# Two-layer attention, scan and expert kernel: the scan's weights prepared inside the first chunk's preparation, and a later LayerNorm in the first feed-forward

## The chip, the cores and the metric

The kernel runs on one core of one Trainium2 chip. The metric is device time in microseconds of one launch, the median of several runs. A core has five engines with queues of their own: PE (matmul; PEld is its weight load), DVE (vector), ACT (activations), POOL (GpSimd) and SP, which here only issues DMAs. Each runs its own instruction list in order, and semaphores tie them together.

## The reference, cut to what matters

```python
x = L0_attn_x                                   # (2, 4096, 256)
xn = layernorm(x)
s = attention(xn)                               # one head of 256
g = silu(ffn(xn))                               # 1024 hidden, sign weights times alpha, gelu
x = x + s * g
xn = layernorm(x)
# the scan: h = exp(delta*A)*h + delta*u*B ; y = sum_n h*C, 64 states, 128 channels
y = layernorm(xn) * ln_gamma + ln_beta
left, right = split(y @ W_up + b_up)
left = silu(causal_conv(left))
s = xn + (s6(left) * silu(right)) @ W_down + b_down
# experts: every expert takes its 512 best tokens of 4096, plus a shared expert for all
g = silu(experts(xn) + shared_expert(xn))
x = x + s * g
```

Matrix products run on values split in a high and a low part (three products for one), so each weight is split too.

## The kernel before

The program is a chain of stages, each ended on all five queues by a fence (`Fence`: every queue drains and waits for the others; SP first waits for its DMAs to land): first feed-forward of batch 0 (fence 1), attention of batch 0 (fence 2), the same for batch 1 (fences 3 and 4), the scan's weights (fence 5), the second layer (fence 6), the final combination.

**The first feed-forward** works on groups of 512 tokens. The order of every queue comes from one counter n in `ffn0_order`, one step for each block of 128 hidden units, eight steps for a group; `load(G, s)` is the preparation of group G at its own step s, which runs 22 steps ahead of the group, so s falls on the step (s + 2) mod 8 of the eight. At s = 0 SP loads x. The statistics come at s = 2, 3, 4, 5 (one block of 128 tokens each, line 467), the root on POOL at 6, the normalising (`apply`, line 475) at 9 and 10, POOL's copies (`keep`) at 11, the two rounds of transposes at 13 and 17 with the copies and remainders one and two steps behind (`xt_lo` line 488, `k_lo` line 492). Of a finished group, `after` has DVE's two scalings by alpha (line 513) at steps 3 and 4 of the eight, and POOL's bias (line 548) at step 5. Each hidden block goes PE (line 575), ACT gelu (line 622), ACT upper part (line 615), DVE lower part `h_lo` (line 497), PE output product; three banks hold hidden blocks, so PE's product for block H needs `h_lo` of H - 3. In batch 0 the weights' own preparation is put at steps of the same counter (`LOW_AT`, `M_AT`, `ALPHA1_AT` and so on); ACT's first gelu waits for alpha1, which DVE makes from w1 (lines 322 and 325).

**The scan's weights** (`scan_weights_sync`, `_scalar`, `_gpsimd`, `_tensor`, `_vector`, lines 1070 to 1132) are 16 small loads on SP, one exponential on ACT, a selection matrix on POOL, eight tiny matmuls (beta through W_up) on PE and 18 operations on DVE (taps of the convolution, gamma into W_up, high and low parts).

**The second layer** merges two threads on every queue, the scan and the experts. `layer1_steps` takes one step of the scan and then, on average, `pace.rate` steps of the experts. The scan is `prepare(0)` with 38 steps, and then a loop of 519 turns of two steps each, one turn for one pair of states of one chunk of 512 tokens (an item; 32 items make a chunk, 512 items all). An item is two recurrences (DVE, line 1427), one read-out (DVE, line 1434), two decays (ACT, line 1743), a drive (POOL, line 1514), a broadcast of C (PE, line 1598) and the sum over states (PE, line 1607, two matmuls twice). The preparation of later chunks runs beside the loop. The experts take 3 steps of preparation, 16 shared blocks of 512 tokens started 19 steps apart and 48 steps long, 109 steps of choosing (rate 1.3), then 32 routed blocks of the same shape. A block has transposes at its steps 7 and 8, gate logits at 13 (shared blocks only), gate products at 17 to 20, gelus after them on ACT, up products at 29 to 35 (DVE's `product`, line 2207, four of a block) and down products at 40 to 44. Both threads fill the same two PSUM banks (`layer_bank`) in PE's order.

The rates before are 1.06 for the shared blocks and 1.07 for the routed ones. The experts' preparation on SP loads the three shared weights (six loads of 512 KB), then the gate's weights, then x of block 0; on POOL the split of the gate's weights stands in `prepare` of `moe_gpsimd`, ahead of the scan's LayerNorm root.

## Time and profile before

| | us |
|---|---|
| runs | 5074.54, 5084.83, 5075.91 |
| median | 5075.91 |
| the profiled execution: its time | 5073.2 |
| its span, first to last instruction | 5071.5 |

| engine | busy us | share of the span |
|---|---|---|
| PE | 4421.6 | 87% |
| DVE | 3596.5 | 71% |
| POOL | 2536.6 | 50% |
| ACT | 2522.1 | 50% |

By the timeline the feed-forwards run from 0 to about 180 us and from 1051 to about 1220, the attentions behind them up to 1047 and 2076, the scan's weights from 2078 to 2093, the scan's first preparation from there to 2171, the loop from there to 4968, the combination to 5071. Busy shares are averages over these stages, which have different limits, so each edit has to be read from its own stage. Busy time of PE overlaps the next matmul's start and is not PE at its peak.

### The profile page before, as it was taken

To read this page: it belongs to the slowest core of one execution; us is meant where nothing else is said; L and a number is where in the kernel's file an instruction comes from. 1 tells how busy PE (TensorE), PEld (TensorE's weight loads), DVE (VectorE), ACT (ScalarE), POOL (GpSimd) and SP (SyncE) were. 2 spreads that over 40 slices of the span, in tenths; PEclk is the share of its full clock that TensorE was granted. 3 is DMA by queue.
4 is the path that set the end of the run, shared out by engine and by line. 5 is a ranking of instruction groups with operands and counts; after the bars stand their busy time and mean duration, and the time that the engine had idled before them with its cause. 6 is when DMAs were issued, how large, how long until landed. Compare 5 with 4: busy or idle time off the path is not lost. (4 is left out here: it accounts for less than half of the span.)

```text
span 5071.5 us, 63742 instructions
## 1 busy us (share of the span) xinstructions
PE 4421.6 (87%) x22534; PEld 3243.6 (64%) x22534; DVE 3596.5 (71%) x5059; ACT 2522.1 (50%) x4773; POOL 2536.6 (50%) x1838
## 2 busy tenths in 40 slices
PE   7899999968999999599999747789998899998972
PEld 6788888857888888466666424556665566665530
DVE  6466666654666666378777899888878778877795
ACT  5544444445444444366666422256665566566542
POOL 3122222232222200166655616788888889888870
PEclk9999999988999999799999968899999999999996
DMA  2022222220122200144333311265555555655546
GB/s 77 33 83 84 84 84 83 78 75 32 67 84 84 79 22 22 55 141 139 126 125 128 126 37 64 77 191 159 173 172 175 148 165 173 186 158 159 141 155 277
DMA packets 270465, 573.15 MB, mean 113 GB/s; under 512 B 37185, under 2 KB 156226, under 8 KB 270146
## 3 DMA queue, kind: packets, MB, share of 16 engines
q1 hardware_dynamic: 245570, 535.51, 31.5%
q0 software_dynamic: 24576, 33.57, 3.8%
q8 instruction: 178, 2.92, 0.2%
q14 instruction: 141, 1.16, 0.1%
HBM read 446.16 MB, written 122.81 MB: 112 GB/s over the span
## 5 line engine op out<-in xcount | busy, mean ns | idle before, releaser
L1514 POOL TENSOR_TENSOR scan_drive_sb<-scan_b_wide_sb,scan_du_sb 128x1024 f32<-128x1024 f32 x512 | 1289.8, 2547 | 450.8 <-DVE scan_h_sb L1427 438.0
L1427 DVE TENSOR_TENSOR_SCAN scan_h_sb<-decay_bank,scan_state_sb,scan_drive_sb 128x512 f32<-128x512 f32 x896 | 1116.6, 1268 | 105.2 <-ACT decay_bank L1743 104.8
L1607 PE MATMUL y_bank<-scan_ch_sb,identity_sb 128*128 128x512 f32 x2048 | 1082.3, 623 | 0.4 <-DVE scan_temp_sb L1440 0.4
L1743 ACT ACTIVATE decay_bank<-scan_delta_sb,a_neg_sb 128x512 f32<-128x512 f32 x1024 | 701.2, 687 | 496.8 <-DVE scan_h_sb L1427 494.3
L1434 DVE TENSOR_TENSOR scan_ch_sb<-c_pair,scan_h_sb 128x1024 f32<-128x1024 f32 x512 | 615.4, 1202 | 136.2 <-PE c_pair L1598 135.4
L957 PE MATMUL ybank<-v_low_hi_lo_sb,pt_hi_b_sb 128*128 128x384 f32 x2048 | 663.3, 358 | 21.9 <-DVE pt_lo_b_sb L837 16.0
L837 DVE TENSOR_TENSOR pt_lo_b_sb<-pt,pt_hi_b_sb 128x512 fp32r<-128x512 f32 x512 | 352.9, 690 | 413.8 <-ACT pt_hi_b_sb L1000 413.8
L958 PE MATMUL ybank<-v_low_hi_lo_sb,pt_lo_b_sb 128*128 128x256 f32 x2048 | 572.3, 279 | 0.0
L991 ACT ACTIVATE p_b_sb<-scores,softmax_cols_b_sb 128x1024 f32<-128x1024 f32 x256 | 286.0, 1117 | 550.2 <-DVE softmax_cols_b_sb L831 410.8
L1598 PE MATMUL c_pair<-scan_cc_sb,select_state_sb 128*128 128x512 f32 x1024 | 386.9, 460 | 147.0 <-DVE scan_ch_sb L1434 145.5
L1000 ACT ACTIVATE pt_hi_b_sb<-pt 128x512 fp32r<-128x512 f32 x512 | 306.1, 598 | 413.6 <-PE pt L945 413.6
L1607 PEld LDWEIGHTS y_bank<-scan_ch_sb,identity_sb 128*128 128x128 f32 x2048 | 391.3, 198 | 142.6 <-issue 72.9
L957 PEld LDWEIGHTS ybank<-v_low_hi_lo_sb,pt_hi_b_sb 128*128 128x128 f32 x2048 | 383.7, 187 | 92.2 <-DVE pt_lo_b_sb L837 80.9
L958 PEld LDWEIGHTS ybank<-v_low_hi_lo_sb,pt_lo_b_sb 128*128 128x128 f32 x2048 | 385.3, 188 | 0.0
L1598 PEld LDWEIGHTS c_pair<-scan_cc_sb,select_state_sb 128*128 128x128 f32 x1024 | 178.5, 199 | 290.0 <-DVE scan_ch_sb L1434 249.7
L900 POOL TENSOR_TENSOR acc_b_sb<-acc_b_sb,g_in_b_sb 128x256 f32<-128x256 f32 x64 | 47.4, 741 | 631.4 <-DVE acc_b_sb L873 631.4
L945 PE MATMUL pt<-identity_sb,p_b_sb 128*128 128x128 f32 x2048 | 316.4, 277 | 14.5 <-ACT p_b_sb L991 13.7
L945 PEld LDWEIGHTS pt<-identity_sb,p_b_sb 128*128 128x128 f32 x2048 | 240.9, 140 | 135.0 <-ACT p_b_sb L991 89.4
L825 DVE TENSOR_REDUCE softmax_cols_b_sb<-scores 128x1 f32<-128x1024 f32 x256 | 310.7, 1214 | 8.9 <-PE scores L924 8.9
L2371 PE MATMUL layer_bank<-moe_xt_hi_sb,expert_hi_sb 128*128 128x512 f32 x512 | 294.3, 575 | 16.4 <-DVE scan_yt_lo_sb L1382 8.4
L2118 POOL TENSOR_TENSOR moe_h_lo_sb<-moe_g_sb,moe_h_hi_sb 128x512 fp32r<-128x512 f32 x192 | 266.3, 1389 | 64.5 <-ACT moe_h_hi_sb L2049 64.5
L2166 POOL DMA_INDIRECT moe_scratch<-moe_out_sb,moe_rows_sb x128 | 204.9, 1601 | 110.5 <-ACT moe_out_sb L2073 81.5
(313 smaller groups left out, 9762.1 us busy)
## 6 DMA issues: line engine op xcount, KB each, us to landing
scan_b_wide_sb<-b_scratch SPq DMA_DIRECT2D x512, 512.0 KB
w_hi_scratch<-split_hi_sb SPq DMA_DIRECT2D x51, 512.0 KB, 2.8
w_lo_scratch<-split_lo_sb SPq DMA_DIRECT2D x51, 512.0 KB, 4.1
expert_hi_sb<-w_hi_scratch SPq DMA_DIRECT2D x48, 512.0 KB
expert_lo_sb<-w_lo_scratch SPq DMA_DIRECT2D x48, 512.0 KB
x_b_sb<-x SPq DMA_DIRECT2D x16, 512.0 KB, 3.9
g_scratch<-g_out_b_sb SPq DMA_DIRECT2D x16, 512.0 KB, 3.0
split_raw_sb<-WgT SPq DMA_DIRECT2D x16, 512.0 KB, 5.2
```

The source lines that it names most:

```text
L825: e.tensor_reduce(v[:, 0, c:c + 1], k.scores[i % 2][:, :], AX_X, ALU.max, negate=True).then_inc(k.s_chunk_max, 1)
L837: e.tensor_tensor(k.pt_lo[n % 2][:, :], k.pt[n % 2][:, :], f32(k.pt_hi[n % 2][:, :]), ALU.subtract).then_inc(k.s_pt_lo, 1)
L945: turned = e.transpose(k.pt[n % 2][:, j * P:(j + 1) * P], k.p[i % 2][:, kb * P:(kb + 1) * P], consts.identity[:, :])
L957: e.matmul(k.y_bank[:, 0:D + P], k.pt_hi[n % 2][:, cols], kv.v[:, block, :], start=(kb == 0), stop=False, skip_group_check=True)
L958: last = e.matmul(k.y_bank[:, 0:D], k.pt_lo[n % 2][:, cols], kv.v[:, block, 0:D], start=False, stop=(kb == KEY_BLOCKS - 1), skip_group_che ...
L1000: e.activation(k.pt_hi[n % 2][:, :], k.pt[n % 2][:, :], ACT.Copy).then_inc(k.s_pt_hi, 1)
L1427: e.tensor_tensor_scan(k.h[i % H_BUFFERS][:, j, :], k.decay_banks[S % DECAY_BANKS][:, :], k.drive[i % DRIVE_BUFFERS][:, j, :], start, ALU. ...
L1434: e.tensor_tensor(k.ch[i % CH_BUFFERS][:, :, :], k.c_bank[:, :, :], k.h[i % H_BUFFERS][:, :, :], ALU.mult).then_inc(k.s_ch, 1)
L1514: e.tensor_tensor(k.drive[i % DRIVE_BUFFERS][:, :, :], k.b_wide[i % B_BUFFERS][:, :, :], k.du[c % 2][:, :].unsqueeze(1).broadcast_to([P, P ...
L1598: last = e.matmul(k.c_bank[:, j, :], wt.select[:, n:n + 1].broadcast_to([P, P]), k.cc[c % 2][:, :], start=True, stop=True)
L1607: e.matmul(k.y_bank[:, :], consts.identity[:, :], k.ch[i % CH_BUFFERS][:, j, :], start=(n == 0), stop=(n == STATES - 1)).then_inc(k.s_y, 1)
L1743: e.activation(k.decay_banks[S % DECAY_BANKS][:, :], k.delta[c % 2][:, :], ACT.Exp, scale=wt.a[:, n:n + 1]).then_inc(k.s_decay, 1)
```

## The change

In the first feed-forward the LayerNorm of a group is done later and in two pieces instead of four; of batch 0, three steps of the weights' preparation move, alpha1 among them, seven steps ahead. The fence behind the scan's weights goes; their loads are issued at the scan's step 1, behind x of chunk 0, the gate's weights, x of block 0 and the first shared weight; POOL's part stands at step 0, PE's and ACT's at step 9, DVE's at step 10, with a new semaphore `s_made` on which PE's first W_up product and ACT's first use of b_up wait. While chunk 0 is prepared, each step of the scan is followed by two steps of the experts, not 1.06: 76 in all instead of 40. The rates behind it become 1.0. The raw weights get room of their own. POOL splits the gate's weights at step 11 of block 0.

```diff
-LN_STATS_AT = (2, 3, 4, 5)
-LN_RSTD_AT = 6
-LN_APPLY_AT = (9, 10)
-KEEP_AT = 11
-TURN0_AT = 13
+LN_STATS_AT = (8, 9)
+LN_RSTD_AT = 10
+LN_APPLY_AT = (12, 13)
+KEEP_AT = 13
+TURN0_AT = 14
-LOW_AT = -15
-M_AT = -14
+LOW_AT = -13
+M_AT = -12
-ALPHA1_AT = -2
+ALPHA1_AT = -9
...
+WEIGHTS_AT = 9
+def after_part(c, s, leads=False):
+    if c > 0:
+        return 1
+    if leads:
+        return 2
+    return 1 if s == 0 else 3 if s == PREPARE_STEPS - 1 else 2
...
     def prepare(c):
         for s in range(PREPARE_STEPS):
+            if c == 0 and s == WEIGHTS_AT + 1:
+                scan_weights_vector(e, w, wt, k.y_bank, consts)
...
-            yield
+            yield from no_steps(after_part(c, s))
...
-SHARED_RATE = 1.06
-MOE_RATE = 1.07
+SHARED_RATE = 1.0
+MOE_RATE = 1.0
...
     def prepare():
+        e.dma_start(k.gate_raw[:, :, :], a["gateT"].rearrange("(c p) n -> p c n", p=P)).then_inc(k.s_gate_raw, 16)
+        load(0)
         for kind in range(3):
             for half, slot in enumerate((k.ws_hi[kind], k.ws_lo[kind])):
                 e.dma_start(f32(slot[:, :]), w_dram[half][3 * EXPERTS + kind]).then_inc(k.s_ws[kind], 16)
             yield
-        e.dma_start(k.gate_raw[:, :, :], a["gateT"].rearrange("(c p) n -> p c n", p=P)).then_inc(k.s_gate_raw, 16)
...
     def shared(q, s):
+        if q == 0 and s == LOGITS_AT - 2:
+            gate_weights()
...
-            scan_weights_vector(e, w, w1, y_bank, consts)
+            layer1_steps(scan_vector(e, w, scan, fills, w1, consts), moe_vector(e, w, moe, fills, pace), pace)
             fence.compute(e, w, 5)
-            layer1_steps(scan_vector(e, w, scan, fills, w1), moe_vector(e, w, moe, fills, pace), pace)
-            fence.compute(e, w, 6)
```

## Rows read from the trace of the kernel before

**Rows 1.** Timeline, batch 1 of the feed-forward: start us, length us, instruction, [idle before].

```profile
1112.96 0.40 PE L575 MATMUL ffn_bank<-xt_hi_b_sb,sign_sb 128*128 128x512 f32 x1
...
1114.72 2.80 DVE L475 TENSOR_SCALAR x_b_sb<-x_b_sb,ln_moments_sb,ln_rstd_sb 128x256 f32<-128x256 f32 x2
...
1114.84 0.40 PE L575 MATMUL ffn_bank<-xt_hi_b_sb,sign_sb 128*128 128x512 f32 x1
...
1114.89 2.48 POOL L548 TENSOR_TENSOR g_out_b_sb<-g_out_b_sb,b_sb 128x1024 f32<-128x1024 f32 x1 [8.04 <-DVE g_out_b_sb L513]
...
1118.91 0.51 PE L575 MATMUL ffn_bank<-xt_hi_b_sb,sign_sb 128*128 128x512 f32 x1 [2.03 <-DVE h_lo_b_sb L497]
```

**Rows 2.** One line's instructions, line 475: duration ns min/median/max, first and last start.

```profile
L475 DVE TENSOR_SCALAR x_b_sb<-x_b_sb,ln_moments_sb,ln_rstd_sb x64: 394/405/2478, 9.2 to 1179.1; 128x256 f32<-128x256 f32 x64
```

**Rows 3.** Waits by total, whole span: total us, times, longest.

```profile
PE ffn_bank L575 <- DVE h_lo_b_sb L497: 37.4, 18, 3.3
```

**Rows 4.** Timeline, the first 30 us, batch 0: PE, ACT, DVE and SP.

```profile
22.95 0.78 PE L575 MATMUL ffn_bank<-xt_hi_b_sb,sign_sb 128*128 128x512 f32 x1
...
25.68 1.28 ACT L622 ACT_TABLE_LOAD   x1 [6.20 <-DVE alpha_sb L325]
...
17.00 0.67 DVE L488 TENSOR_TENSOR xt_lo_b_sb<-ffn_bank,xt_hi_b_sb 128x512 fp32r<-128x512 f32 x1
...
23.06 2.31 DVE L322 TENSOR_REDUCE alpha_sb<-g_out_b_sb 128x4 f32<-128x1024 f32 x2
...
29.92 0.69 DVE L497 TENSOR_TENSOR h_lo_b_sb<-ffn_bank,h_hi_b_sb 128x512 fp32r<-128x512 f32 x1 [3.80 <-ACT h_hi_b_sb L615]
...
3.75 2.06 SPq L297 DMA_DIRECT2D b_sb<-b  x1
```

**Rows 5.** DMA issues, 0 to 20 us: count, KB each, median us from issue to landing.

```profile
b_sb<-b SPq DMA_DIRECT2D x1, 4.0 KB, 9.6
```

**Rows 6.** Timeline around the fences: SP, POOL and PE.

```profile
2078.01 0.38 SPq L1074 DMA_DIRECT2D gamma_sb<-ln_gamma  x1
...
2093.03 0.38 SPq L1332 DMA_DIRECT2D scan_xn_sb<-xn_scratch  x1
...
2105.02 0.22 POOL L2110 TENSOR_SCALAR gate_hi_sb<-gate_raw_sb 128x32 fp32r<-128x32 f32 x1 [26.11 <-DMA gate_raw_sb<-gateT]
...
2109.94 1.09 PE L1542 MATMUL layer_bank<-identity_sb,scan_xn_sb 128*128 128x128 f32 x4 [20.77 <-ACT scan_xn_sb L1639]
```

**Rows 7.** Busy us of each engine by stretch (count), then PE's granted clock, DMA share, GB/s.

```profile
2078.00:2093.00 15.00, 1.84 (x8) 1.78 (x8) 4.46 (x16) 0.26 (x1) 0.62 (x3) 0.50 0.20 42
2093.00:2171.00 78.00, 45.93 (x213) 35.26 (x214) 11.01 (x25) 38.27 (x76) 22.02 (x20) 0.72 0.29 100
2200.00:2800.00 600.00, 569.05 (x2459) 390.80 (x2458) 466.21 (x478) 386.93 (x820) 363.92 (x205) 0.96 0.40 129
...
3400.00:4800.00 1400.00, 1289.26 (x5199) 852.73 (x5198) 1114.53 (x1116) 874.06 (x1610) 1195.20 (x736) 0.97 0.56 166
4860.00:4968.00 108.00, 78.35 (x203) 34.75 (x204) 106.41 (x93) 43.91 (x89) 67.59 (x30) 1.00 0.40 134
```

**Rows 8.** Groups by line, 2200 to 2800 us: count, busy us, mean ns, idle before.

```profile
L1607 PE MATMUL y_bank<-scan_ch_sb,identity_sb 128*128 128x512 f32 x446 | 236.5, 616 | 0.0
L1434 DVE TENSOR_TENSOR scan_ch_sb<-c_pair,scan_h_sb 128x1024 f32<-128x1024 f32 x112 | 134.9, 1204 | 33.6 <-PE c_pair L1598 33.5
...
L1598 PE MATMUL c_pair<-scan_cc_sb,select_state_sb 128*128 128x512 f32 x222 | 86.3, 472 | 5.5 <-DVE scan_ch_sb L1434 5.2
...
L2207 DVE TENSOR_TENSOR moe_g_sb<-layer_bank,moe_g_sb 128x512 f32<-128x512 f32 x48 | 32.8, 684 | 26.1 <-PE layer_bank L2373 25.7
```

**Rows 9.** Groups by line, 3400 to 4800 us, DVE.

```profile
L1434 DVE TENSOR_TENSOR scan_ch_sb<-c_pair,scan_h_sb 128x1024 f32<-128x1024 f32 x268 | 322.5, 1203 | 98.1 <-PE c_pair L1598 97.3 <-DVE scan_h_sb L1427 0.4
```

**Rows 10.** Groups by line, 4860 to 4968 us, the end of the loop.

```profile
L1434 DVE TENSOR_TENSOR scan_ch_sb<-c_pair,scan_h_sb 128x1024 f32<-128x1024 f32 x30 | 35.8, 1194 | 0.0
```

**Rows 11.** Timeline, DVE, 2150 to 2172 us: the first recurrence.

```profile
2171.18 3.45 DVE L1427 TENSOR_TENSOR_SCAN scan_h_sb<-decay_bank,scan_drive_sb 128x512 f32<-128x512 f32 x3 [11.62 <-ACT decay_bank L1743]
```

More of the change, by code:

```diff
@@ L462, in ffn0_vector, with statistics @@
 def ffn0_vector(e, w, k, wt, kv, b):
-    def statistics(G, j):
+    def statistics(G, half):
         x = k.x[G % X_BUFFERS]
@@ L478, in load @@
     def load(G, s):
-        j, half = part(LN_STATS_AT, s), part(LN_APPLY_AT, s)
-        if j is not None:
-            statistics(G, j)
+        first, half = part(LN_STATS_AT, s), part(LN_APPLY_AT, s)
+        if first is not None:
+            statistics(G, first)
         if half is not None:
@@ L1059, in __init__ @@
         self.s_scaled = self.sem("gamma_in_up")
[L1060 to L1066 removed]
+        self.s_made = self.sem("made")
+        self.raw_up = self.sb("up_raw", [P, DC, D])
+        self.raw_delta = self.sb("wdelta_raw", [P, INNER])
+        self.raw_bc = self.sb("bc_raw", [P, 2, 2, STATES])
+        self.raw_down = self.sb("down_raw", [P, D])
+        self.raw_select = self.sb("select_raw", [P, STATES])
 def scan_weights_sync(e, w, k, a):
@@ L1131, in scan_weights_vector @@
     w.wait_ge(k.s_select, 3)
-    e.tensor_copy(k.select[:, :], k.raw_select[:, :])
+    e.tensor_copy(k.select[:, :], k.raw_select[:, :]).then_inc(k.s_made, 1)
 class Fills(Stage):
@@ L1416, in prepare @@
                 c_lower(c)
-            yield
+            yield from no_steps(after_part(c, s))
     def recur(S):
@@ L1493, in prepare @@
         for s in range(PREPARE_STEPS):
+            if c == 0 and s == 0:
+                scan_weights_gpsimd(e, w, wt)
             if s == STATISTICS_AT[1] + 1:
@@ L1506, in prepare @@
                 delta_u(c)
-            yield
+            yield from no_steps(after_part(c, s))
     def drive(i):
@@ L1547, in up @@
             fills.wait_emptied(w, "turned", c, ci)
+        w.wait_ge(wt.s_made, 1)
         bank = fills.take(w, what, c)
@@ L1574, in prepare @@
         for s in range(PREPARE_STEPS):
+            if c == 0 and s == WEIGHTS_AT:
+                scan_weights_tensor(e, w, wt, k.y_bank)
             ci = part(TURNED_AT, s)
@@ L1589, in prepare @@
                 b_and_c(c, 1)
-            yield
+            yield from no_steps(after_part(c, s, True))
     def broadcast_c(i):
@@ L1656, in left @@
         fills.wait_filled(w, "left", c)
+        w.wait_ge(wt.s_made, 1)
         w.wait_ge(k.s_head, c - c // CHUNKS)
@@ L1713, in prepare @@
         for s in range(PREPARE_STEPS):
+            if c == 0 and s == WEIGHTS_AT:
+                scan_weights_scalar(e, w, wt)
             half, ci = part(APPLY_AT, s), part(TURNED_AT, s - 1)
@@ L1736, in prepare @@
                 c_upper(c)
-            yield
+            yield from no_steps(after_part(c, s))
     def decay(S):
@@ L1926, in shared @@
     def shared(q, s):
-        if s == 0:
+        if s == 0 and q > 0:
             load(q)
@@ L2181, in routed @@
             scatter(q, j)
-    yield from moe_order(pace, prepare(), shared, choose(), routed)
+    yield from moe_order(pace, prepare_steps(), shared, choose(), routed)
 def moe_vector(e, w, k, fills, pace):
@@ L2589, in scalar @@
                 fence.compute(e, w, 2 + 2 * b)
-            scan_weights_scalar(e, w, w1)
+            layer1_steps(scan_scalar(e, w, scan, fills, w1), moe_scalar(e, w, moe, fills, pace), pace)
             fence.compute(e, w, 5)
-            layer1_steps(scan_scalar(e, w, scan, fills, w1), moe_scalar(e, w, moe, fills, pace), pace)
-            fence.compute(e, w, 6)
             combine_scalar(e, w, combine)
@@ L2616, in gpsimd @@
                 fence.compute(e, w, 2 + 2 * b)
-            scan_weights_gpsimd(e, w, w1)
+            layer1_steps(scan_gpsimd(e, w, scan, fills, w1, consts), moe_gpsimd(e, w, moe, fills, consts, pace, xn_dram, acc_dram), pace)
             fence.compute(e, w, 5)
-            layer1_steps(scan_gpsimd(e, w, scan, fills, w1, consts), moe_gpsimd(e, w, moe, fills, consts, pace, xn_dram, acc_dram), pace)
-            fence.compute(e, w, 6)
         def sync(e):
```

48 lines of the change are left out of this document (20 added, 28 removed).

## The prediction, made before the changed kernel ran

> **What bounds the kernel now.** I read three views in this order. The timeline around each edited place shows what waits for what. The busy time by stretch [rows 7] shows what each stage is bound by. The groups by line in the same stretches [rows 8 to 10] give how many items and blocks go through.
>
> In the first feed-forward PE should run without a pause and waits 18 times for `h_lo`, 37.4 us in all [rows 3]. One such wait is in rows 1: DVE's second pair of normalisings, two instructions, takes 2.80 us from 1114.72, while POOL's bias runs from 1114.89 to 1117.37. The pair ends 0.15 us behind POOL's instruction, `h_lo` stands behind it on DVE, and PE idles 2.03 us. The usual time of one normalising is 0.405 us, the longest 2.478 [rows 2].
>
> Between 2078.0, when the fence behind the attention opens, and 2109.9, PE does eight tiny matmuls [rows 6, 7]. The scan's weights take 15.0 us of it. Then POOL's split of the gate's weights waits until 2105.02 for a load that SP issued behind six loads of 512 KB, and the LayerNorm of chunk 0 is queued behind that split. From 2093 to 2171 PE is busy 45.9 us of 78. The first recurrence starts at 2171.18, behind a wait of 11.62 us for ACT's decay [rows 11].
>
> In the loop beside shared experts (2200 to 2800) PE is busy 95% and DVE 78%; beside routed ones (3400 to 4800) PE 92%, POOL 85%, DVE 80%; in the tail, where the experts are done, DVE 99% [rows 7]. One item takes 600/112 = 5.36 us, 1400/268 = 5.22 us and 108/30 = 3.6 us there [rows 7 to 10].
>
> **Part 1: LayerNorm order.** Nothing is added or removed; operations move on DVE, POOL, ACT and PE. Normalising was on steps 3 and 4 of the eight, right behind the alpha scaling whose end releases POOL's bias. It goes to steps 6 and 7. A step is 1.88 us where PE is full: its hidden products start at 1112.96 and 1114.84 [rows 1]. The bias starts about 1.3 us into step 4 (behind `h_lo` and the scaling, 0.6 us each) and lasts 2.48, so it ends near 3.8 us; the first normalising comes behind `h_lo` of step 6, at 3.76 + 0.6 = 4.4 us. It clears by half a microsecond. The long form occurs ten times, five in each batch, as in rows 1, and the PE waits behind them are four of 2.0 to 2.1 and one of 1.3 in either batch: 19.1 us in all, of the 37.4 in rows 3.
>
> What is late next: statistics now stand in pairs (1.06 us) on steps 2 and 3, beside `xt_lo` (0.6) and a scaling (0.6). With `h_lo` (0.6) DVE has 2.26 us for a step of 1.88 twice in a row, so `h_lo` is 0.4 and then 0.8 us late. The path from PE through both ACT operations and `h_lo` back to PE has about 0.5 us to spare (one and a half steps, 2.8 us, against 2.3). I put 0.35 us on each of some 14 groups: 5 us back. Net -14; bounds 0 back (-19) and 0.8 us for each group (-8). The silu pairs, other causes of waits in rows 3, stay.
>
> The lock on SBUF ports weighs here. The Trainium skill ("SBUF — State Buffer", section "SBUF: two separate sides") says that DVE's two-port modes and GpSimd share one port pair as an exclusive lock, and that whichever starts first holds it for its whole instruction. The rows above agree with that; by this rule the half microsecond of clearance decides, and if the bias still starts first the gain of part 1 is zero instead of 14 (a rival below).
>
> **Start of batch 0.** PE's first hidden product starts at 22.95 and ACT's first gelu only at 25.68, when alpha1 is made; the first `h_lo` is at 29.92 [rows 4]. DVE made alpha1 from 23.06 because that is its place in the order; its last input landed at 3.75 + 9.6 = 13.3 us [rows 4, 5]. Moved, it runs from 13.4 to 15.9. It holds back `xt_lo` of group 0, which could start at 14.3 but in the old order ran at 17.0 behind statistics of group 1 that waited for x; now it ends at 16.6 instead of 17.7. Then two statistics, `k_lo` at 19.3, and PE's first product near 19.4. Behind it stand the transposes of group 1, now one step later, waiting for its normalising at 21.7. The third gelu comes 3 us earlier. I take -3, bounds 0 and -4.5. In batch 1, where alpha1 exists and x is the only wait, the product starts some 2 us earlier but the transposes behind it take that back: 0, within 1. Part 1 in all: -17, from -8 to -22.
>
> **Part 2: fence, weights and double pace.** Removed: a fence, and 15 us in which nothing but the weights ran [rows 7]. Added to the preparation: the same 16 loads on SP (issues of 0.45 us each, 7.5 us), ahead of only two of the three shared weights, which block 0 needs at its steps 29 and 40, far later; and the weights' 18 DVE operations, 4.5 us busy, on an engine that is busy 11 of 78 us there. New waits: PE stands at its step 9 until the last load lands, about 2090, with the logits of block 0 already done; `s_made` is set near 2096 and PE needs it at step 15, after 2100. Both are short. SP's xn load moves from 2093.0 to 2078.0, and gate weights no longer wait for 3 MB, so PE's first work, transposes of block 0, can start near 2083 instead of 2109.9.
>
> The experts' steps done by the first recurrence go from 48 to 84: 36 steps, 36/19 = 1.9 blocks. PE's price of a block: of 569 us busy in the shared stretch, items take 236.5 + 86.3; the rest is 246 us for 48/4 = 12 blocks, 20.5 us each [rows 7, 8]. So PE's work in the preparation is 45.9 + 1.9 x 20.5 = 85 us. Before, PE started at 2110 and idled 15 us up to 2171. With the same 15 us of idle time the first recurrence comes at 2083 + 85 + 15 = 2183. No idle time gives 2168, idle time that grows with the work (28 us) 2196. I take 2182, +11 on 2171, bounds -3 and +25. The scan is late and the experts are ahead.
>
> **Part 3: what that is worth in the loop.** Let a be what one more item costs while experts run beside it. A shared block with its 19/1.06/2 = 8.96 items costs 8.96 x 5.36 = 48.0 us, so a block alone 48.0 - 8.96a. Taking 1.9 blocks out saves 91.0 - 17.0a. The loop steps beside experts are counted from the schedule. Shared: before 336/1.06 - 38 = 279 steps (139.5 items), after 336 - 76 = 260 (130). Choosing: 109/1.3 = 84 (42 items) in both. Routed: before 637/1.07 = 595 (297.7 items), after 637 (318.5). Together 479 items before, 490.5 after: 11.4 items move from the tail, at 3.6 us, to a. The sum is 11.4(a - 3.6) - (91.0 - 17.0a) = 28.4a - 132.
>
> For a there are two near rows. If PE sets the pace, a is an item's PE time, (236.5 + 86.3)/112 = 2.88 us [rows 8]: -50. If DVE does, it is the tail's 3.6 [rows 7, 10]: -30. PE is fuller in both stretches, but the 20% idle time of DVE is partly a wait for the broadcast (97 us in 1400, rows 9), and POOL at 85% is near. I take 3.3: -38. The Trainium skill ("Perfetto Trace Analysis", section "Identifying the Most-Contended Engine") calls matmul busy time a poor measure of PE's load and takes weight-load time instead. That is 65% and 61% in these stretches, so PE would not be the limit and DVE's 3.6 would stand. The time by that is 5040; I give it a quarter of the forecast's chance, since PE's waits in rows 8 are short.
>
> **Sum.** -17 + 11 - 38 = -44 on the profiled execution's 5073.2 (span 5071.5): 5029. The median of the runs lies 2.7 us above it, so I forecast 5032.
>
> **Rivals.**
>
> A. Slower: the loop's order, not an engine's load, sets the time of a step, so that an item beside experts costs the same 5.36 us whatever fewer expert steps it carries. With a = 5.36 part 3 is +20 and the time 5076 + 20 + 11 - 17 = 5090. The place is the routed stretch, with 20.8 items more at 5.22 against the tail's 3.6. It decides from a = 4.86 on (28.4a - 132 + 11 - 17 = 0), where the sum is zero. Against it: no row shows an idle PE there (92 to 95%), which a fixed step time needs. For it: ACT and DVE waits for each other on every second item. Chance 0.09.
>
> B. The collision of normalising and bias only moves: `h_lo` late on steps 2 and 3 pushes the bias into step 6. Part 1 gives -3 instead of -17: 5046. For it: clearance of 0.5 us. Against: PE's pace sets both steps. Chance 0.14.
>
> C. The preparation is bound by ACT, not PE: 38 us busy of 78 before, and 1.9 blocks more bring up to 1.9 x 387/12 = 61 us [rows 7], with a table load of 1.28 us at each change of function [rows 4] beside the softplus. PE would idle 23 us more than I allow: first recurrence at 2205, +34 instead of +11, 5055. Chance 0.15.
>
> D. The rates of 1.0 spread the experts' work evenly and PE's stalls fall: 1% of 2100 us, 5011. It is in the forecast's own range. The forecast with it holds 0.62.
>
> **How the numbers follow.** Best ends: -22 - 3 - 50 = -75, 5000. Worst ends: -8 + 25 - 30 = -13, 5063. From 4998 to 5063 the range leaves out A and a part of C. The measurement tells a difference from 0.2%, 10 us, so faster means below 5066: the forecast, B and most of C, 0.87. Same: 0.05. Slower: 0.08, nearly all of A.
>
> **What the profile would show.** Line 475 has no duration over 1 us between 60 and 180 us and between 1090 and 1200, and PE's wait for `h_lo` falls from 37 to about 20 us; if the maximum stays near 2.5, B holds. The first `h_lo` is near 27. SP's xn load comes right behind the fence at about 2060 (part 1 earlier), PE's first expert transposes 5 us behind it, and the first recurrence 104 us behind the fence instead of 93. Over 120 it is C. In the loop an item takes about 5.2 us in the shared stretch and 5.1 in the routed one (fewer expert steps each); if both stay at 5.36 and 5.22, it is A. The last expert product is followed by about 30 items instead of 42. The prediction is wrong if a is outside 2.9 to 3.6, or if the even rate meets the scan's order badly, which no row can show.

## The result, and the profile after

The changed kernel takes 5009.39 us (median, 5004.19 to 5017.5), the kernel before 5080.37 beside it (5074.54 to 5090.1): a ratio of 0.986, 95% interval 0.9836 to 0.9884, or 71 us. I had forecast 5032, in a range from 4998 to 5063. The profiled execution took 5004.19 (span 5002.3) against 5073.2 (span 5071.5): 69 us for the two profiles, with which I compare below.

The first feed-forward. One line's instructions (duration ns min/median/max) and, from the waits of the whole span (total us, times, longest), PE's wait for `h_lo`:

```profile
L476 DVE TENSOR_SCALAR x_b_sb<-x_b_sb,ln_moments_sb,ln_rstd_sb x64: 402/407/414, 9.3 to 1162.3; 128x256 f32<-128x256 f32 x64
...
PE ffn_bank L576 <- DVE h_lo_b_sb L498: 19.6, 9, 3.3
```

Line 476 is the normalising, line 475 before. Its longest was 2478 ns [rows 2] and is now 414; PE's wait for `h_lo` fell from 37.4 us in 18 pauses [rows 3] to 19.6 in 9. The timeline shows the new order of a group, with the place of the bias in it:

```profile
1101.05 0.68 DVE L514 TENSOR_TENSOR g_out_b_sb<-ffn_bank,alpha_sb 128x512 f32<-128x512 f32 x1
...
1101.96 2.42 POOL L549 TENSOR_TENSOR g_out_b_sb<-g_out_b_sb,b_sb 128x1024 f32<-128x1024 f32 x1
...
1104.52 0.73 DVE L476 TENSOR_SCALAR x_b_sb<-x_b_sb,ln_moments_sb,ln_rstd_sb 128x256 f32<-128x256 f32 x2
```

The bias ends at 1104.38, 0.14 us ahead of the normalising; over the ten groups in which the two are neighbours the distance is 0.10 to 0.52 us. In rows 1 the two began 0.17 us apart. PE's busy time between the first and the last `h_lo` of batch 1, before and after (columns as in rows 7: start and end, length, busy us of PE, PEld, DVE, ACT, POOL, then the granted clock):

```profile
1074.30:1221.10 146.80, 128.64 (x792) 115.10 (x792) 87.59 (x155) 101.00 (x157) 45.63 (x47) 0.95 0.12 37
```

```profile
1061.10:1196.80 135.70, 124.67 (x792) 111.06 (x792) 79.04 (x164) 101.99 (x159) 47.03 (x50) 0.99 0.13 40
```

The same 792 matmuls take 4 us less of busy time, at a granted clock of 0.99 and not 0.95. At the start of batch 0 (the views of rows 4, here of the changed kernel) alpha1 is made from 13.43 and the first `h_lo` comes at 25.79 instead of 29.92:

```profile
13.43 2.34 DVE L322 TENSOR_REDUCE alpha_sb<-g_out_b_sb 128x4 f32<-128x1024 f32 x2 [2.72 <-DMA b_sb<-b]
...
19.35 0.80 PE L576 MATMUL ffn_bank<-xt_hi_b_sb,sign_sb 128*128 128x512 f32 x1 [1.59 <-DVE k_lo_sb L493]
...
25.79 0.69 DVE L498 TENSOR_TENSOR h_lo_b_sb<-ffn_bank,h_hi_b_sb 128x512 fp32r<-128x512 f32 x1 [4.21 <-ACT h_hi_b_sb L616]
```

The preparation, timeline of SP, POOL, PE and DVE (the views of rows 6 and 11):

```profile
2054.35 0.37 SPq L1345 DMA_DIRECT2D scan_xn_sb<-xn_scratch  x1
...
2056.85 0.45 SPq L1074 DMA_DIRECT2D gamma_sb<-ln_gamma  x1
...
2062.52 0.22 POOL L2135 TENSOR_SCALAR gate_hi_sb<-gate_raw_sb 128x32 fp32r<-128x32 f32 x1
...
2059.82 1.94 PE L2360 MATMUL layer_bank<-identity_sb,moe_x_sb 128*128 128x128 f32 x8 [11.69 <-DMA moe_x_sb<-xn_scratch]
...
2175.81 2.34 DVE L1444 TENSOR_TENSOR_SCAN scan_h_sb<-decay_bank,scan_drive_sb 128x512 f32<-128x512 f32 x2 [10.94 <-ACT decay_bank L1768]
```

SP's first issue behind the attention comes at 2054.35 instead of 2078.01, POOL's split of the gate's weights no longer waits 26 us for its load, and PE's first transposes come 5.5 us behind SP's first issue, not 32. But the first recurrence comes 121.5 us behind that issue, where it had been 93.2. By stretch (columns as in rows 7: length, busy us of PE, PEld, DVE, ACT, POOL, then the granted clock): the preparation, the shared stretch, the routed one and the tail:

```profile
2054.00:2176.00 122.00, 94.23 (x459) 77.05 (x459) 25.68 (x58) 66.12 (x141) 32.69 (x31) 0.84 0.27 89
2200.00:2800.00 600.00, 562.48 (x2395) 383.21 (x2394) 477.20 (x491) 385.40 (x812) 376.62 (x213) 0.97 0.40 130
3400.00:4780.00 1380.00, 1282.46 (x5161) 839.51 (x5160) 1145.31 (x1135) 883.66 (x1629) 1210.77 (x741) 0.98 0.57 170
4803.00:4898.00 95.00, 67.89 (x173) 29.59 (x172) 92.41 (x80) 38.99 (x80) 59.87 (x26) 1.00 0.41 134
```

Groups by line for the read-out of an item, in 2200 to 2800, 3400 to 4800 and 4803 to 4898 us (the views of rows 8 to 10): 115 items instead of 112, 283 instead of 268, and DVE's idle time in front of them 71.2 us in the routed stretch instead of 98.1.

```profile
L1451 DVE TENSOR_TENSOR scan_ch_sb<-c_pair,scan_h_sb 128x1024 f32<-128x1024 f32 x115 | 138.5, 1204 | 36.2 <-PE c_pair L1620 36.1
...
L1451 DVE TENSOR_TENSOR scan_ch_sb<-c_pair,scan_h_sb 128x1024 f32<-128x1024 f32 x283 | 340.3, 1202 | 71.2 <-PE c_pair L1620 70.7
...
L1451 DVE TENSOR_TENSOR scan_ch_sb<-c_pair,scan_h_sb 128x1024 f32<-128x1024 f32 x27 | 32.1, 1190 | 1.1 <-PE c_pair L1620 1.1
```

**Every stage of every run.** The table is read from the timelines. "FFN" is from the first to the last `h_lo`, both batches added. "Fence" is SP's first issue behind the last attention, "prep" from there to the first recurrence. The loop is cut where ACT empties the last bank of the shared experts, and the first and the last of the routed ones; behind the stroke stand the items read out in that stretch. "Tail" is the rest of the 512 items. All in us, one profiled execution each.

| kernel | first h_lo | FFN | fence | prep | shared | choosing | routed | tail | span |
|---|---|---|---|---|---|---|---|---|---|
| before | 29.9 | 298.2 | 2078.0 | 93.2 | 712 / 134 | 506 / 63 | 1444 / 276 | 135 / 39 | 5071.5 |
| after | 25.8 | 278.9 | 2054.4 | 121.5 | 644 / 124 | 519 / 64 | 1464 / 296 | 96 / 28 | 5002.3 |
| e1_ln_only | 25.0 | 281.7 | 2056.7 | 93.0 | 714 / 134 | 507 / 63 | 1444 / 276 | 135 / 39 | 5053.2 |
| e2_rates_only | 29.8 | 299.2 | 2083.2 | 98.6 | 738 / 143 | 510 / 64 | 1457 / 296 | 27 / 9 | 5018.2 |
| e3_old_rates | 25.9 | 280.4 | 2057.5 | 127.6 | 602 / 115 | 506 / 63 | 1445 / 276 | 210 / 58 | 5052.2 |
| e4_moe_092 | 24.9 | 285.1 | 2061.9 | 121.9 | 643 / 124 | 524 / 66 | 1538 / 322 | none | 4992.6 |
| e5_uneven | 25.8 | 280.4 | 2057.2 | 122.8 | 646 / 124 | 517 / 64 | 1493 / 296 | 96 / 28 | 5035.7 |
| e6_moe_103 | 25.6 | 282.8 | 2059.4 | 125.9 | 646 / 124 | 517 / 64 | 1450 / 287 | 127 / 37 | 5030.9 |
| e7_moe_096 | 25.8 | 284.9 | 2062.0 | 123.9 | 646 / 124 | 524 / 65 | 1508 / 309 | 45 / 14 | 5013.1 |
| e8_collide | 25.7 | 286.4 | 2066.1 | 124.2 | 643 / 124 | 519 / 64 | 1467 / 296 | 96 / 28 | 5020.1 |
| e9_collide_bias | 25.8 | 334.4 | 2110.1 | 124.5 | 643 / 124 | 516 / 64 | 1470 / 296 | 96 / 28 | 5064.0 |
| e10_single_pace | 25.4 | 282.7 | 2057.2 | 82.0 | 741 / 143 | 510 / 64 | 1456 / 296 | 27 / 9 | 4978.4 |
| e11_alpha_late | 26.7 | 286.2 | 2062.4 | 124.3 | 646 / 124 | 517 / 64 | 1470 / 296 | 96 / 28 | 5018.9 |
| e12_warm | 25.8 | 282.7 | 2058.9 | 119.6 | 645 / 124 | 516 / 64 | 1467 / 296 | 96 / 28 | 5006.1 |

How far one profile can be trusted is in the table too: the feed-forward of the changed order, identical in eight of the kernels (after, e3 to e7, e10, e12), lasts 278.9 to 285.1 us, the fence of the old order comes at 2078.0 in before and at 2083.2 in e2, and the preparation at double pace 119.6 to 127.6 (the longest at the rate of 1.06, with 4 expert steps more in it). A difference under 5 us in one stage means nothing.

Against before, the loop gained 68 in the shared stretch and 39 in the tail, and lost 13 in the choosing and 20 in the routed stretch: 74 us. The feed-forwards and the start gave 24, and the preparation took 28.

### The profile page after: what moved, and what is told of

Read it like the earlier page. It is cut to its first block and busy times, and to the rows that moved or that the text cites. A ratio compares the mean times of both kernels' runs of the same rounds, so it can differ in the third digit from the quotient of the medians.

```text
span 5002.3 us, 63736 instructions
## 1 busy us (share of the span) xinstructions
PE 4413.1 (88%) x22534; PEld 3233.9 (65%) x22534; DVE 3570.6 (71%) x5059; ACT 2524.3 (50%) x4773; POOL 2539.3 (51%) x1838
## 5 line engine op out<-in xcount | busy, mean ns | idle before, releaser
L889 POOL TENSOR_SCALAR split_hi_sb<-split_raw_sb 128x512 fp32r<-128x512 f32 x102 | 63.5, 622 | 388.8 <-DMA split_raw_sb<-WgT 123.6
```

## The experiments

Each was timed against the kernel before on the same chip. Medians in us; the intervals of the ratio are 95%.

| kernel | median | ratio to before | interval |
|---|---|---|---|
| e1_ln_only | 5060.13 | 0.9956 | 0.9939 to 0.9973 |
| e2_rates_only | 5028.47 | 0.9903 | 0.9886 to 0.9919 |
| e3_old_rates | 5053.08 | 0.9946 | 0.993 to 0.9963 |
| e4_moe_092 | 4998.23 | 0.9843 | 0.9826 to 0.9859 |
| e5_uneven | 5038.28 | 0.9913 | 0.9896 to 0.9929 |
| e6_moe_103 | 5030.35 | 0.9897 | 0.9881 to 0.9914 |
| e7_moe_096 | 5010.5 | 0.9855 | 0.9838 to 0.9871 |
| e8_collide | 5021.52 | 0.9877 | 0.986 to 0.9893 |
| e9_collide_bias | 5059.81 | 0.9945 | 0.9929 to 0.9962 |
| e10_single_pace | 4980.64 | 0.9793 | 0.9777 to 0.9809 |
| e11_alpha_late | 5015.65 | 0.9858 | 0.9841 to 0.9875 |
| e12_warm | 5008.44 | 0.9852 | 0.9835 to 0.9868 |

The profile of after left two theories to tell apart. The feed-forward had gained 24 us and not 17: was the collision of the normalising with POOL's bias its cause at all? And the routed stretch had taken 20 items more for 20 us, where I had put 3.3 us on each: was that the rate, or something that came with the preparation?

### Part by part

**e1_ln_only**: the first three blocks of the diff and the pair statistics, on the kernel before.

```diff
-LN_STATS_AT = (2, 3, 4, 5)
+LN_STATS_AT = (8, 9)
...
-LN_APPLY_AT = (9, 10)
+LN_APPLY_AT = (12, 13)
...
-ALPHA1_AT = -2
+ALPHA1_AT = -9
```

> The kernel before with the LayerNorm order alone (statistics in pairs, normalising on steps 6 and 7, transposes a step later, the start of the alphas). If part 1 is independent of the rest, the whole of the 24 us by which the attention of batch 1 ended earlier in the changed kernel comes back here: attention ends at 2038 to 2039, the total is 24 us below the kernel before, 5049 on a profiled 5073. If the gain of the later parts leans on it, or if the 24 us hold something of the other parts, it is the predicted 17 or less.

The fence comes 21 us earlier and nothing behind it changes (preparation 93.0, the loop's stretches within 2 us). The time falls by 0.44%, 22 us (18 between the profiles). Part 1 is independent of the rest, and 24 us is the upper end of what one profile shows: over the profiles with this order the fence lies 16 to 24 us ahead of before's 2078.0.

**e2_rates_only**: on the kernel before.

```diff
-SHARED_RATE = 1.06
-MOE_RATE = 1.07
+SHARED_RATE = 1.0
+MOE_RATE = 1.0
```

> The kernel before with both rates at 1.0, everything else as it was. Shared: 298 steps instead of 279, 9.5 items more; routed 637 instead of 595, 20.8 more; the tail 30.3 fewer at 3.5 us. As predicted (one more item beside experts costs 3.3 us whatever the stretch): -6 to -9 us in all. By what the changed kernel's milestones show (20 routed items more at 1.0 us each): shared -3, routed and tail 20.8 x (1.0 - 3.5) = -52, together -55. If the low price needs the preparation or the weights of the changed kernel, it is near the first number.

It gives 0.97%, 49 us (53 between the profiles), near the second of the two forecasts. So two constants bring over two thirds of the change's gain, without the preparation or the weights. The shared stretch takes 9 items more for 26 us, 2.8 each; the routed one 20 more for 13, 0.65 each; the tail, 30 fewer, is 108 us shorter, 3.6 for each. By this the shared rate is worth some 7 us and the routed one some 59; `SHARED_RATE` alone was not run.

**e3_old_rates**: the reverse edit on the changed kernel.

> The changed kernel with the rates of before, 1.06 and 1.07. The reverse of the run with the rates alone: +6 to +9 us on the changed kernel if an item beside experts costs 3.3 us (5015), +55 if a routed one costs 1.0 us (5062). The preparation stays as it is in the changed kernel, first recurrence at 2176, since its steps do not hang on the rate of the stretch that follows, apart from one block's steps.

5053, with the routed stretch back at 1445 us for 276 items. The profile also isolates part 2: this kernel is e1 with the weights and the double pace inside, and the two spans are 5053.2 and 5052.2. The preparation is 34.6 us longer, the shared stretch 112 shorter with 19 items fewer, the tail 76 longer with the same 19 items. All of part 2 together is worth nothing that can be measured at these rates (ratios 0.9956 and 0.9946). The reverse edit costs 0.86%, 44 us, between its two forecasts of 6 to 9 and 55.

### What a routed item costs

**e4_moe_092, e6_moe_103, e7_moe_096**: `MOE_RATE` alone, on the changed kernel.

```diff
-MOE_RATE = 1.0
+MOE_RATE = 0.92
```

> The changed kernel with the routed rate at 0.92 instead of 1.0: 637/0.92/2 = 346 items beside routed experts instead of 318, 28 more, and none left in the tail. Smooth price of 1.0 us for an item more (the time is in the experts' steps, items are nearly free): 28 x (1.0 - 3.4) = -67 us on the changed kernel, 4940. Price of 3.3 us as predicted: -3, 5004. Even rate theory (only a whole number of expert steps for each item avoids stalls, at 1.0 exactly, worth the 48 us by which the routed stretch beat the forecast): the stalls come back, +48 - 3 = +45, 5052.

> The changed kernel with the routed rate 1.03: 637/1.03/2 = 309 items instead of 318.5, 9.3 fewer beside routed experts and as many more in the tail. Linear between 1.07 and 1.0 (either a fixed loss for each step with two expert steps, or a bound by the experts' own chain): routed stretch 1464 - 9.3 x 0.9 = 1456, tail +32, kernel about +24 on the changed one, 5033. If only exactly 1.0 is good (the order of items and expert steps in a fixed phase): 1464 - 28 + 48 = 1484, kernel about +52, 5061. At one price of 3.3 us: +1.

> The changed kernel with the routed rate 0.96: 637/0.96/2 = 332 items, 13.3 more beside routed experts, 13.3 fewer in the tail of 28. Between 1.0 and 0.92 the stretch grew by 74 us for 26 items, 2.85 each. On that line: 1464 + 38 = 1502, tail -45, kernel -7, 5002. If leaving exactly 1.0 costs a fixed amount and the line from there is flatter, the stretch is above 1510 and the kernel above the changed one, over 5010.

The routed stretch by rate: 1.07, 1444 us with 276 items; 1.03, 1450 with 287; 1.0, 1464 with 296; 0.96, 1508 with 309; 0.92, 1538 with 322. Below 1.0 an item more costs (1538 - 1464)/26 = 2.85 us. That is PE's work for an item, 2.88 by rows 8, the lower of my two ends. (If the steps without an expert step, which come with a rate below 1.0, cost something too, the item itself costs less than 2.85.) Above 1.0 it seems to cost only (1464 - 1444)/20 = 1.0. The price of nearly nothing, on which e4 should have gained 67 us, falls with e4 (11 us, and its interval overlaps that of the changed kernel). So does "only exactly 1.0 is good", with e6: its stretch would have been 1484, and there were 1450, with the kernel at 5030 where the straight line gave 5033. One price of 3.3 us falls with e6 as well, since by it the kernel would have moved by 1 us and it moved by 21. e7 does not decide its question: 1508 us and 5010.5 lie between the straight line (1502 and 5002) and a fixed loss for leaving 1.0 (above 1510 and 5010), and the difference is no more than one profile and one interval (8 us to either side) can tell.

**e5_uneven**: the same mean rate beside routed experts, unevenly dealt.

```diff
     for _ in scan:
         due += pace.rate
+        if pace.n is not None:
+            due += (pace.n % 14 == 3) - (pace.n % 14 == 10)
+            pace.n += 1
```

(`pace.n` is set to 0 where the routed experts begin.)

> The changed kernel, mean rate 1.0 beside routed experts, but unevenly: of every 14 scan steps one carries two expert steps and another, seven steps later, none (45 of either). Number of items and of expert steps beside each other stay as in the changed kernel. If it is the even order that made the routed stretch cheap (a step with two expert steps stalls, 42 of them at 1.07, 20 x 3.0 - 20 = 40 to 48 us lost there, about 1 us each), the stretch of 1464 us grows by 40 to 48 us and the kernel to about 5055. If it is the mean rate alone (with more expert steps for each item their own chain sets the pace and an item is nearly free, with fewer it is PE), it stays within 10 us of 1464 and the kernel within 10 of the changed one, 5009. As predicted, with one price of 3.3 us: no change either, but that leaves the run with the rates alone unexplained.

The stretch takes 1493 us for the same 296 items, 29.5 more than in after (1456 to 1470 in the kernels with an even 1.0, so 23 to 37 more), and the median is 29 us higher: less than the 40 to 48 expected, and far from none. So unevenness by itself costs: 45 steps with two expert steps and 45 with none, 29.5 us, about 0.66 for each pair. How much of it belongs to the doubled steps, no run shows. My estimate gives them all of it, because the skipped ones don't show by themselves: at 0.92 there are 55 of them, and the items still cost PE's 2.85. At 1.07 there are 42 doubled steps, 42 x 0.66 = 28 us, and at 1.03 18.5 of them, 12 us. With that taken off, an item costs (20 + 28)/20 = 2.4 us from 1.07 to 1.0, and (14 + 12)/9 = 2.9 from 1.03 to 1.0. By this estimate the low price was the sum of a normal one and a loss that ended. Some 8 to 10 us of the 1.07 stretch are not explained by it. Nor does the shared stretch bear it out: from 1.06 to 1.0, with some 15 doubled steps fewer, 9 items more took 26 us in e2, and 42 from e3 to after (about 5 of them for four expert steps that stood in e3's preparation), where a loss that ended should have made them cheap.

Where it is lost, the waits show (DVE's read-out waiting for PE's broadcast, 3440 to 4800 us; total us, times, longest), in the order before, after, e5:

```profile
DVE scan_ch_sb L1434 <- PE c_pair L1598: 96.3, 57, 9.6
```

```profile
DVE scan_ch_sb L1451 <- PE c_pair L1620: 66.6, 50, 4.0
```

```profile
DVE scan_ch_sb L1451 <- PE c_pair L1620: 74.8, 46, 5.0
```

The broadcast stands on PE's queue behind the expert step, or behind two. In e5 the waits grow less than the time, so this row shows the direction and not the whole of the 29.5.

### The collision

**e8_collide**: the alpha scalings onto the steps of the normalisings.

```diff
-SCALE_AT = (FFN_LAG + 1, FFN_LAG + 2)
-BIAS_AT = FFN_LAG + 3
-GATES_AT = FFN_LAG + 5
+SCALE_AT = (FFN_LAG + 4, FFN_LAG + 5)
+BIAS_AT = FFN_LAG + 6
+GATES_AT = FFN_LAG + 8
```

> The changed kernel with the two alpha scalings moved from steps 3 and 4 of the eight to steps 6 and 7, onto the normalisings, the bias and the silu behind them three steps later as well: the neighbours of the kernel before in the order of the change. If it is the overlap of normalising and bias that stretched the normalising from 0.4 to 2.5 us: long normalisings come back, about ten of them, PE's waits for the lower half of h grow by about 19 us, the first feed-forwards end 19 us later in all, kernel about 5028. If the gain came from the pair statistics or from the later transposes: no long normalisings, within 5 us of 5009.

No normalising is longer than 414 ns. The edit had missed: POOL's copies of the normalised x stood ahead of the bias, so the bias came after the normalising and not beside it. It serves as the control: the steps moved, no overlap, and FFN 286.4. That is 7.5 us above after at the same granted clock of 0.99, 6 of it in PE's pauses (30 us against 24), so moving the steps costs a little by itself.

**e9_collide_bias**: the same, with the bias one step earlier (`BIAS_AT = FFN_LAG + 5`, `GATES_AT = FFN_LAG + 7`), which puts it ahead of POOL's copies.

> As the run before with the scalings on steps 6 and 7, but with POOL's bias queued ahead of POOL's copies of the normalised x (there it stood behind them, and no normalising overlapped with a bias). Now the bias is released by the second scaling and starts beside the second pair of normalisings, as in the kernel before. Overlap as the cause: normalisings of over 2 us come back in most of the 16 groups, and PE's wait for the lower half of h rises from 19.6 us to 39 or more; both feed-forwards together last 279 us in the changed kernel and would last 298 or more here, kernel about 5030 to 5040. Pair statistics or later transposes as the cause: no normalising over 1 us or no longer waits behind them, under 285 us, within 5 us of the run before, 5021.

```profile
L476 DVE TENSOR_SCALAR x_b_sb<-x_b_sb,ln_moments_sb,ln_rstd_sb x64: 402/406/2432, 9.3 to 1213.2; 128x256 f32<-128x256 f32 x64
```

```profile
1138.70 2.75 DVE L476 TENSOR_SCALAR x_b_sb<-x_b_sb,ln_moments_sb,ln_rstd_sb 128x256 f32<-128x256 f32 x2
...
1138.87 2.44 POOL L549 TENSOR_TENSOR g_out_b_sb<-g_out_b_sb,b_sb 128x1024 f32<-128x1024 f32 x1 [5.76 <-DVE g_out_b_sb L514]
...
1141.51 1.05 PE L563 MATMUL ffn_bank<-identity_sb,x_b_sb 128*128 128x128 f32 x4 [2.54 <-DVE x_b_sb L476]
...
1142.21 0.78 PE L576 MATMUL ffn_bank<-xt_hi_b_sb,sign_sb 128*128 128x512 f32 x1
```

Batch 1 between the first and the last `h_lo`, in e8 and in e9 (columns as above):

```profile
1067.70:1207.10 139.40, 125.33 (x792) 111.22 (x792) 78.10 (x163) 101.92 (x159) 44.28 (x49) 0.99 0.12 38
```

```profile
1089.10:1251.10 162.00, 135.81 (x792) 120.79 (x792) 88.06 (x163) 102.26 (x159) 44.85 (x49) 0.91 0.11 33
```

Ten long normalisings are back, five in each batch, as before, and they look like rows 1: the pair starts 0.17 us ahead of the bias and ends 0.14 behind it. Against e8 the bias and the silu behind it are one step earlier and POOL's copies come behind the bias; only then is there an overlap, and the feed-forwards last 48 us longer (38 by the medians, 5059.81 against 5021.52; the profiled run of e9 took 5065.85). The long normalisings come from the overlap: e8 has none, e9 has ten, each beside a bias. The price was wrong in my expectation, in two ways. PE now waits for the normalised x itself (2.54 here), since its transposes follow at once, and hardly for `h_lo`: its pauses grow by 24 us over both batches. And its busy time for the same matmuls grows by 24 us too (10.5 in the batch shown, 13.8 in the other), because the granted clock falls from 0.99 to 0.91 and 0.88: behind the pause of 2.54 us a hidden product of 128x512 lasts 0.78 us, where it is 0.39 ahead of it. So a collision costs 4 to 5 us in this order, half of it in the clock; in the order before it was some 2.

**e11_alpha_late**: `ALPHA1_AT = -2` on the changed kernel.

> The changed kernel with the first alpha made at its old place, step -2 instead of -9. If the early start of batch 0 comes from it (first lower half of h at 25.8 instead of 29.9), it goes back to 29 to 30 and all milestones behind it are 3 to 4 us later; with statistics and normalising in the new order alone the start is within 1 us of 25.8 otherwise. Kernel +3 or 0: below what the times can tell, so the milestones decide.

The first `h_lo` is at 26.7, not 29 to 30. Alpha1 is made from 19.27 here, since the statistics of group 1 no longer stand between it and the start, and PE's first product starts at 17.78, earlier than after's 19.35:

```profile
17.78 0.79 PE L576 MATMUL ffn_bank<-xt_hi_b_sb,sign_sb 128*128 128x512 f32 x1 [2.56 <-DVE k_lo_sb L493]
...
19.27 2.34 DVE L322 TENSOR_REDUCE alpha_sb<-g_out_b_sb 128x4 f32<-128x1024 f32 x2
```

Of the 4 us at the start, alpha's move gives about 1 (the first `h_lo` comes at 24.9 to 25.9 in the kernels that have it), and the rest of part 1 the other 3: the LayerNorm order with the two weight steps `LOW_AT` and `M_AT`, which were not run apart.

### The preparation

**e10_single_pace**: the weights stay in the preparation, the double pace goes.

```diff
 def after_part(c, s, leads=False):
-    if c > 0:
+    if c >= 0:
         return 1
```

> The changed kernel with one expert step for each step of chunk 0's preparation, as before; the weights stay inside it. 38 expert steps fewer beside the preparation, 2 blocks. Preparation from the end of attention to the first recurrence: 137 us in the changed kernel, 109 before. If the double pace is what lengthened it (PE work of 2 blocks, 16 to 20 us each), it falls to 100 to 105, some 4 to 9 below before because the weights no longer stand alone; the shared stretch grows by 38 steps, 19 items, at 5.2 = about +100, and the tail falls by 19 items, -67. Kernel within 8 us of the changed one (5009), since the double pace as a whole gave about nothing in the runs of part 1 alone against the changed kernel with the old rates. If the double pace is worth what I predicted (35 in the loop less 11 to 15 in the preparation): 5029 to 5033.

Both forecasts missed (5009 within 8 us, 5029 to 5033). This is the fastest kernel of the study, 4980.64: 2.07% below before, with an interval (0.9777 to 0.9809) that doesn't touch that of the changed kernel (0.9836 to 0.9884). The double pace costs about 30 us (24 between the profiles, 34 by the ratios). Its balance by the table: preparation +39.5, choosing +9, routed +8, tail +69, shared -97, that is +28. (My expectations count the preparation from the end of the attention's own work, 15.5 us ahead of SP's first issue: their 137 us is the table's 121.5.) And the rest of part 2 without double pace, the weights inside the preparation and the new order of loads, gains 11 us: 82.0 against 93.2, or 16.6 against e2's 98.6 at the same rate. At the rates of before e3 and e1 differ by nothing, so by this account the double pace cost only some 10 us there; why it costs more at 1.0 is not shown. The preparation and the tail of this kernel (columns as above):

```profile
2057.00:2139.00 82.00, 46.07 (x203) 35.24 (x203) 15.20 (x41) 37.77 (x75) 22.60 (x23) 0.70 0.32 106
...
4847.00:4872.00 25.00, 18.00 (x45) 7.64 (x43) 25.00 (x22) 9.52 (x22) 14.65 (x7) 1.00 0.27 74
```

PE is busy 46.1 of 82 us here and 94.2 of 122 with double pace. DVE is busy all of the 25 us in the tail. Two blocks more in the preparation are 48 us of busy time and 40 us of time: they filled 8 of the 36 idle us, and the rest was paid in full, 20 us a block. In the loop the same two blocks, with their 19 items, take 97 us, and the 19 items alone in the tail 69: 28, 14 us a block. That is what the two engines say: beside a block, 9.5 items cost PE's 20.5 + 9.5 x 2.88 = 47.9 us (measured 97/2 = 48.4), and alone they cost DVE's 9.5 x 3.6 = 34. The loop has room on PE, since its items alone are bound by DVE; the preparation is a chain in which PE waits for what ACT and DVE take out of its two banks (8 and 10 us in after's 122), with little room that a queue in a fixed order can use.

**e12_warm**: PE is kept busy between the fence and the experts' first transposes.

```diff
+            if c == 0 and s == 0:
+                for _ in range(16):
+                    e.matmul(k.y_bank[:, 0:P], consts.identity[:, :], consts.identity[:, :], start=True, stop=True)
```

> The changed kernel with 16 matmuls of 128 columns put on PE right behind the fence, into the bank of y, whose result nobody reads; PE idles there for some 5 us in the changed kernel. The granted clock in the changed kernel is 0.50 to 0.53 from the fence to 20 us behind it, while PE is busy 12.4 of 18 us, and single matmuls take about twice their time. If the low clock is what makes the preparation longer than I predicted, the clock is near 1.0 in this stretch from the sixth microsecond on and the preparation of 137 us becomes 129 to 132. If waits for banks and for ACT set the pace, the clock rises and the preparation stays at 136 to 141.

24 us in after and in e12, from 2.5 us behind SP's first issue on (columns as above; the clock is the sixth figure behind the length). In e12 the fillers run from 2058.84 to 2064.77:

```profile
2056.90:2062.90 6.00, 1.94 (x8) 1.57 (x8) 3.25 (x10) 1.50 (x3) 1.99 (x6) 0.50 1.03 304
2062.90:2068.90 6.00, 5.63 (x27) 5.67 (x27) 0.56 (x4) 2.04 (x6) 0.18 (x1) 0.50 0.74 236
2068.90:2074.90 6.00, 4.84 (x17) 3.73 (x16) 4.26 (x16) 1.87 (x12) 0.00 (x0) 0.61 1.01 358
2074.90:2080.90 6.00, 4.59 (x15) 3.50 (x16) 1.39 (x3) 2.31 (x5) 0.00 (x0) 0.72 0.08 27
```

```profile
2061.40:2067.40 6.00, 4.46 (x30) 4.03 (x29) 2.42 (x9) 0.96 (x2) 1.94 (x6) 0.85 1.01 297
2067.40:2073.40 6.00, 4.90 (x30) 4.93 (x30) 1.87 (x7) 3.04 (x12) 0.22 (x1) 0.72 0.84 224
2073.40:2079.40 6.00, 3.92 (x13) 3.04 (x13) 3.71 (x14) 1.87 (x10) 0.00 (x0) 0.71 1.04 387
2079.40:2085.40 6.00, 5.28 (x17) 3.90 (x18) 1.37 (x3) 1.70 (x4) 0.00 (x0) 0.72 0.05 17
```

The clock rose from 0.50, the lower of its two levels, to between 0.71 and 0.85, but the preparation is 119.6 us, 2 below after, and the time unchanged (5008). So the low clock of these 24 us is not what makes the preparation long. The clock near 1.0 that I expected came only for 3 us (1.00 from 2064.4 to 2067.4); in the next window it was 0.72. Over the whole preparation it was 0.87 instead of 0.84, where the loop has 0.97, so the test says little about the rest of the stretch.

## Why the prediction came out as it did

The time lay in the range, 23 us under the forecast, with two errors of opposite sign in it: that the sum came out in the range is in part luck.

**Part 1** (-17, from -22 to -8): right. The mechanism is shown (e8 against e9), line 476 has no long duration, the waits for `h_lo` fell to 19.6 as written. Measured: 22 us by e1's ratio, 16 to 24 by the fences of the profiles. PE's pauses between the first and the last `h_lo` went from 37.4 to 23.8 us in all (3.3 of it for `xt_lo`, which had cost nothing before): 14 less, as forecast. What the forecast had no term for is the clock: the same matmuls took 263 us of busy time at a granted clock of 0.95 before, and 255 at 0.99 after. That part varies from run to run, since e4 has after's order and pauses at 0.95 to 0.96, with 261 us. The forecast's half microsecond of clearance was 0.10 to 0.52 us. The rule of the Trainium skill ("SBUF — State Buffer", section "SBUF: two separate sides") that the one to start first holds the shared ports for its whole instruction agrees with e9's row for the second of the two normalisings: it starts 0.16 us behind the bias, lasts 2.43 us instead of 0.41, and ends 0.14 us behind it. For the first it does not show: that one starts 0.17 us ahead of the bias and takes its usual 0.40, and the bias takes 2.44 us, against 2.42 without an overlap. Rival B is refuted: the collision didn't move. The start's -3 was right in size and wrong in cause: alpha gives 1 of it (e11).

**Part 2** (first recurrence 104 us behind the fence, bound 118): wrong. It is 121.5 in after and 119.6 to 127.6 in all profiles at double pace, 17 us more than forecast and above the bound. In the forecast's own terms, PE's start behind the fence, its work, and its idle time from that start on, the sum was 5 + 85 + 15; measured in after are 5.5 + 94 + 22. Two terms failed. The work: a block was priced at 20.5 us from the shared stretch, where the granted clock is 0.96 [rows 7]; two blocks in the preparation were 48 us of busy time (after against e10), 24 each, at a clock of 0.84. An estimate, 20.5 x 0.96/0.84 = 23.4, says that the clock is most of it; no run tests that. And "with the same 15 us of idle time": I took those 15 us from before's stretch between PE's start at 2110 and 2171, and so counted the earlier start as PE time to be filled by blocks. Without more blocks (e10) the first recurrence comes 82 us behind the fence with 46 us of work: 36 us idle, of which the two blocks filled 8. I never worked out that case, and so didn't see that the double pace had to be paid for. Rival C had the number (over 120), but its reason is not borne out: ACT is busy 66 of 122 us, not the 99 that it needs, PE 94.

**Part 3** (28.4a - 132, a = 3.3: -38, best -50): -74. By stretch the sum was shared -(9.5a + 35) = -66, routed +69, tail -41. Measured: shared -68, tail -39, routed +20, choosing +13 where I had 0. The shared and the tail term were right, and so was the count (28 items in the tail, forecast 30). The term mis-sized is a for the routed items. It stood for two things: the price of an item beside routed experts is near PE's own, at most 2.85 (e4), not 3.3; and by the estimate from e5 about 28 us of the stretch before were a loss by uneven steps, which is rival D. D's time was 5011, by 1% of the loop; it came true in the routed stretch alone, at about 1.9% of it, so that D's time is as near as it is by chance. Rival A is refuted: an item takes 644/124 = 5.19 us in the shared stretch (5.31 before) and 1464/296 = 4.95 in the routed one (5.23 before). The Trainium skill ("Perfetto Trace Analysis", section "Identifying the Most-Contended Engine") judges PE's headroom by weight-load time, and by the share of peak arithmetic, which I did not work out. By weight-load time, 61 to 65%, PE would not be the limit and a would have been 3.6; here the measured 2.85 is near PE's matmul time for an item, 2.88, so matmul busy time was the better measure in this case.

**The sum.** Predicted -17 + 11 - 38 = -44; measured on the profiles -24 + 28 - 74 = -70, and +1 behind the loop.

**What stays open.** The first question is why the choosing takes 516 to 519 us at double pace and 510 at single, with the same 64 items, and the routed stretch 1464 to 1470 instead of 1456: the experts stand at another phase to the scan's chunks, which was not tested by itself. The next is how the 29.5 us of e5 divide between doubled and skipped steps; e4 only suggests that they belong to the doubled ones. It is open too whether a doubled step costs the same at 1.07 as in e5: with a period of 14 steps e5's doubled steps all fall on the same one of a turn's two steps, while those of 1.07 wander. The last is why evenness doesn't show in the shared stretch.

## What to carry to other kernels

Work moved from a loop into its preparation is free only as far as it fills idle time there: compare the busy time that it adds with the length that it adds, and with what it leaves behind in the loop (here 20 us a block paid, 14 saved). Of two merged threads, look at how evenly the steps are dealt as well as at the mean rate: a rate of 1.07 is a doubled step every fourteenth time, and dealing the same steps unevenly cost 29 us (e5). The two rates of 1.0 gave two thirds of this change's gain. And a bundle of edits needs one run for each, since a part that costs 30 us can hide in a sum of -71.

## What the runs showed of the hardware

- The price of a DVE instruction stretched beside one of POOL depends on who stands behind it: ten overlaps of the same 2.4 us cost some 20 us in the order before and 38 to 48 in e9, where PE's transposes follow the normalising directly.
- In e9 short pauses of PE cost twice: ten waits of about 2.5 us for the normalised x and the pauses that follow from them added 24 us of idle time, and another 24 us of busy time for the same matmuls, at a granted clock of 0.88 and 0.91 where e8 had 0.99.
- 5.9 us of filler matmuls on an idle PE left the granted clock at 0.50 for their first 2.5 us; it was 0.69 in the next 3 us and 1.00 in the 3 us after that. In the three windows of 6 us behind it, with PE busy 4.9, 3.9 and 5.3 us, it was 0.71 to 0.72.
